# A ninth seven-product pair in the second row group of a two-group layer-1 product

## The chip, the cores and the metric

The kernel runs on one core of one Trainium2 chip. The metric is the device time of one execution in microseconds (us). A core has five engines that run on their own and wait for each other through semaphores: PE (TensorE, the matrix engine), DVE (VectorE), ACT (ScalarE), POOL (GpSimd) and SP (SyncE, which only issues transfers here). PEld is PE's loading of weights, which overlaps its multiplying. Transfers (DMAs) are issued from SP, and from POOL where they add to what lies at their target.

## The reference, cut to what matters

```python
def layer_norm(x):
    mu = jnp.mean(x, axis=-1, keepdims=True)
    sigma = jnp.sqrt(jnp.mean((x - mu) ** 2, axis=-1, keepdims=True))
    return (x - mu) / sigma
x1, x2 = x[:, :5120], x[:, 5120:]          # x: (1024, 10240)
h1 = leaky_relu(layer_norm(x1 @ W1.T))     # W1: (256, 5120)
h2 = leaky_relu(layer_norm(x2 @ W1.T))
h1 = leaky_relu(layer_norm(h1 @ W2.T))     # W2: (64, 256)
h2 = leaky_relu(layer_norm(h2 @ W2.T))
h = leaky_relu(layer_norm(jnp.concatenate([h1, h2], -1) @ W3.T))   # W3: (8, 128)
y = h @ W4.T                               # W4: (1, 8)
```

Nearly all of the work is the first product, with F = 5120 as the contracted dimension. The rest is called layers 2 to 4 below.

## The kernel before, in words

The rows are cut into two groups of 512. A group has B = 2 blocks of 512 columns b (256 rows times the two halves x1 and x2), W1 has M = 2 blocks of 128 outputs m. The contraction runs over PAIRS = 20 pairs of 128-element slices, so a pair is a 2 by 2 by 2 block product. It is done in one of two ways:

- A unit of kind E does the pair as eight block products. It has two parts (E0, E1), one for each slice, and each needs 4 products.
- A unit of kind S does it as seven (Strassen's way in Winograd's form). It has a part R (three products on blocks as they are loaded: A11, A12, S4 into banks P1, P2, P3) and a part T (four products on sums of blocks: S1, S3, S2, A22 into P5, P7, P6, P4). The sums of x are made on DVE (`two_sums` L758, `third_sum` L767, `fourth_sum` L777) in `x_sum`. For units with `added_by_dma` (L319, the third to the sixth S unit of the whole kernel) the first two of them are made by a DMA from POOL's queue that adds the block b12 to two loaded blocks (`add_b12`, L496).

Each product is made with three matmuls of 128 by 512, since float32 is split in a high and a low part: ACT casts to `_hi` (`hi`, L577), DVE subtracts to `_lo` (`lo`, L707), and PE multiplies hi by hi, lo by hi and hi by lo. An E unit is therefore 24 matmuls, an S unit 21 (R 9, T 12). The split buffers R, T, E0 and E1 are single: ACT casts into one only when PE has used it (`used`).

W1 is centred, summed and split once, in the first group, by ACT and DVE. A pair that is E in the first group and S in the second needs its weights a second time in the summed form. Those units are in `W_WORK` (L125): w is loaded again by SP (L471), centred by ACT (L566), summed by three DVE instructions (L743, L748, L753), cast by ACT (L575) and subtracted by DVE (L717). Before, two units of the second group need it.

The order of the units is written in ORDER (L46). F is the first unit of the second group, L the last of the first group, whose four (b, m) blocks are finished one after another, and D is the last of all, two E pairs in four parts, first for b = 0 and then for b = 1. All engines go through the same order in loops over `RUNS` (L130: a run is the E-like units between two S units, then an S unit). The run that crosses from group to group is written out by hand for ACT (L644) and DVE (L948): DVE adds up the seven products (`seven_into`, L797) and the eight (`eight_into`, L816) into h1, ACT makes the leaky ReLU and the squares (`leak1`, `square1`), PE makes layer 2 (L1152) right after F and layer 3 (L1183) after the unit behind F, ACT squares and casts layer 2's result (`layer2_end`), DVE copies layer 3's and the variances' bank out (`small`, L992), and PE may only start the bank P7 (before) when that copy is made (`free`, L1051). POOL folds the squares with a row of adding DMAs (L509 to L530) and raises to the power -1/2 (`root12`, `root3`); DVE ends the first group beside the unit named by `first_end` (L993).

In the names of units below, S7 is the first S unit of the second group (the seventh of all), S8 the next, and so on. Before, these are S7 to S14; E' is the E unit behind F, and the last units are S14, E, D.

Of the kernel before, what the change touches and what calls it, by code (L numbers as in the profile page):

```python
# [17 lines left out]
B = 2  # L18
# [8 lines left out]
MIXED = 2  # L27
# [7 lines left out]
EARLY = 2  # L35
E_RING = 4
W23_UNIT = 7
# [8 lines left out]
ORDER = ("EHE" + "SEE" * 3 + "SE" * 2 + "SEEL", "FE" + "SE" * 8 + "D")  # L46
# [39 lines left out]
def plan():  # L86
    units, made, halves, sevens = [], {}, 0, 0
    for g, order in enumerate(ORDER):
        seen = {"S": 0, "E": 0}
        for kind in order:  # L90
# [4 lines left out]
            else:  # L95
# [4 lines left out]
                elif kind in "HL":  # L100
                    wanted = [("T", pair, 0, (0, 1)), ("T", pair, 1, (0, 1))]
                elif kind == "D":
                    wanted = [("E0", pair, 0, (0, 1)), ("T", pair + 1, 0, (0, 1)), ("T", pair + 1, 1, (0, 1)),
                              ("E1", pair, 1, (0, 1))]
                else:
                    wanted = [("E0", pair, 0, (0, 1)), ("E1", pair, 1, (0, 1))]
# [15 lines left out]
SEVENS = [u for u in UNITS if u.kind == "S"]  # L122
HALVES = {part.half: part for u in UNITS if u.kind != "S" for part in u.parts}
# [32 lines left out]
def rec_kernel(nc, x, w1, w2, w3, w4, out):  # L156
    with ExitStack() as ctx:  # L157
# [36 lines left out]
        unused = sb("unused", [P, 2, N1], BF16)  # L194
        w2_raw = sb("w2_raw", [P, M, N2])
# [19 lines left out]
        sq3 = sb("sq3", [P, B * T, N3])  # L215
        a3 = sb("a3", [P, B * T, N3])
        weighted = sb("weighted", [P, B * T, N3])
        var3 = sb("var3", [P, B * T])
# [89 lines left out]

        def two_slot(u):


            return u.nth % S_RING, 16 * ((u.nth - EARLY) // S_RING + 1)

        def b12_slot(u):

            n = u.nth if u.nth < EARLY else u.nth - SEVEN + EARLY
            return u.nth % S_RING, 16 * (n // S_RING + 1)

        def added_by_dma(u):  # L319
            return EARLY <= u.nth < SEVEN  # L320
# [41 lines left out]
        def _(sp):  # L362
# [79 lines left out]
            for es, n, after in RUNS:  # L442
# [20 lines left out]
                if es[0].n == W23_UNIT:  # L463
                    sp.dma_start(w2_raw[:], w2).then_inc(small_landed, 16)
# [13 lines left out]
        def _(pool):  # L478
# [25 lines left out]
            for u in SEVENS[EARLY:SEVEN]:  # L504
                add_b12(u)
# [36 lines left out]
        def _(act):  # L542
            def mean(u, c):
                s, landed = w_slot(u)
                act.activation(unused[:, c, :], w_raw[:, s, c * N1:(c + 1) * N1], ACT.Copy, scale=-1.0 / N1,  # L545
# [57 lines left out]
            def layer1_end(g):  # L603
                for b in range(B):
                    for m in range(M):
                        leak1(g, b, m)
                for b in range(B):
                    for m in range(M):
                        square1(g, b, m)

# [27 lines left out]
            for i, (es, n, after) in enumerate(RUNS):  # L638
                if not n:
                    copy_p1(GROUPS - 1)  # L640
                    for part in es[1].parts:
                        hi(es[1], part)
                    break
                if crosses(es):  # L644
# [54 lines left out]
        def _(dve):  # L699
# [67 lines left out]
            def third_sum(u):  # L767
# [4 lines left out]
                else:  # L772
                    dve.wait_ge(two_sums_made, u.nth + 1 if u.nth < EARLY else u.nth + 1 - SEVEN + EARLY)
# [23 lines left out]
            def seven_into(g, k):  # L797
# [7 lines left out]
                if k == 1:  # L805
                    dve.wait_ge(h1_step, 2 * g + 1)
                    dve.tensor_tensor(h1[1][0], h1[1][1], acc[:, P5, :], ALU.add)
# [4 lines left out]
                if k == 3:  # L812
                    dve.wait_ge(h1_step, 2 * g + 2)
# [448 lines left out]
```

## Time and profile before

| | us |
|---|---|
| median of 3 runs | 230.14 |
| lowest and highest | 229.82 and 230.61 |
| the profiled execution | 229.74 |
| its span, from the first to the last instruction | 228.0 |
| PE busy | 222.1 (97%) |
| DVE busy | 193.9 (85%) |
| ACT busy | 152.1 (67%) |
| POOL busy | 27.9 (12%) |

The profiled execution is 229.74 us long, of which 228.0 us are the span and 1.7 us lie around it. Busy time says how long an engine had an instruction in work. For DVE and ACT two neighbouring instructions overlap in the listing by about 0.09 us, so the distance from start to start is what one costs in a row. A matmul is listed with some 0.39 us, but PE starts one every 0.23 us. The profile also has the granted clock of TensorE, which is 0.99 of full speed over the span.

### The profile page before, as it was taken

Reading aid. Unit: us, or ns where it says so; the run is one execution under the profiler, and the core shown is the slowest. Engines: PE = TensorE matmul, PEld = TensorE weight load, DVE = VectorE, ACT = ScalarE, POOL = GpSimd, SP = SyncE. Lnnn points to the kernel's source line nnn. Section 1 sums busy time; section 2 is a strip of 40 time slices with the busy share of each in tenths; the row PEclk is TensorE's granted clock in tenths of the full one; section 3 lists DMA queues with packets and bytes.
Section 4 is the critical chain, followed back from the end, with each engine's and each line's share of the span. In section 5 each row is a group of like instructions: output and inputs, shape, how many; then the busy total and the mean of one; then the engine's idle time right before and its main releaser. Section 6 shows DMA issues by size and latency. Waiting matters only on the chain.

```text
span 228.0 us, 2897 instructions
## 1 busy us (share of the span) xinstructions
PE 222.1 (97%) x991; PEld 178.6 (78%) x991; DVE 193.9 (85%) x264; ACT 152.1 (67%) x240; POOL 27.9 (12%) x41
## 2 busy tenths in 40 slices
PE   8999999999999999999999999999999999999992
PEld 2888877888888888888868888888888888888771
DVE  3789999959779999996669799998989999968564
ACT  4997989689498598963678363665545585616540
POOL 0000020200200200000012243227040000000014
PEclk9999999999999999999999999999999999999996
DMA  6999999999999998546738958567666815050000
GB/s 214 405 407 407 401 358 324 316 242 348 309 216 379 302 312 283 175 157 224 281 66 235 282 196 281 207 213 220 215 212 206 272 75 184 3 184 1 3 0 1
DMA packets 17950, 51.93 MB, mean 228 GB/s; under 512 B 2772, under 2 KB 3156, under 8 KB 17936
## 3 DMA queue, kind: packets, MB, share of 16 engines
q1 hardware_dynamic: 15920, 48.60, 60.7%
q0 software_dynamic: 1872, 2.89, 7.8%
q10 hardware_dynamic: 144, 0.26, 0.4%
q8 instruction: 8, 0.13, 0.2%
q14 instruction: 6, 0.05, 0.1%
HBM read 50.95 MB, written 0.01 MB: 224 GB/s over the span
## 4 chain that ended last, share of the span: by engine, by line
PE 83%; DVE 5%; ACT 4%; DMA 4%; issue 1%; POOL 1%; SPq 1%; POOLq 0%; DVEq 0%
PE acc L1037 80%; DMA xe_raw<-x 4%; PE acc L1158 2%; DVE xe_lo L709 2%; ACT xe_hi L591 2%; ACT unused L545 1%; DVE x_sum L764 1%; ACT xt_hi L591 1%; DVE x_sum L774 1%; ACT we_hi L551 0%; POOL inv L488 0%; PE acc L1171 0%; ACT stage L551 0%; PE acc L1187 0%; POOLq L157 0%
## 5 line engine op out<-in xcount | busy, mean ns | idle before, releaser
L1037 PE MATMUL acc<-xe_lo,we_hi 128*128 128x512 f32 x176 | 68.8, 391 | 0.3 <-DVE xe_lo L709 0.2
L1037 PE MATMUL acc<-xe_hi,we_lo 128*128 128x512 f32 x176 | 68.5, 389 | 0.0
L591 ACT CAST xe_hi<-xe_raw 128x1024 fp32r<-128x1024 f32 (+1 forms) x48 | 48.2, 1011 | 28.2 <-PE acc L1037 22.4
L709 DVE TENSOR_TENSOR xe_lo<-xe_raw,xe_hi 128x1024 fp32r<-128x1024 f32 (+1 forms) x48 | 55.5, 1178 | 12.3 <-ACT xe_hi L591 11.9
L1037 PE MATMUL acc<-xe_hi,we_hi 128*128 128x512 f32 x176 | 48.4, 391 | 0.0
L1037 PEld LDWEIGHTS acc<-xe_lo,we_hi 128*128 128x128 f32 x176 | 33.0, 188 | 8.4 <-issue 1.7
L1037 PEld LDWEIGHTS acc<-xe_hi,we_hi 128*128 128x128 f32 x176 | 32.9, 188 | 7.8 <-issue 1.1
L1037 PEld LDWEIGHTS acc<-xe_hi,we_lo 128*128 128x128 f32 x176 | 33.0, 188 | 6.7
L591 ACT CAST xt_hi<-x_sum 128x2048 fp32r<-128x2048 f32 x14 | 26.8, 1912 | 14.0 <-DVE x_sum L780 14.0
L709 DVE TENSOR_TENSOR xt_lo<-x_sum,xt_hi 128x2048 fp32r<-128x2048 f32 x14 | 32.1, 2290 | 1.9 <-ACT xt_hi L591 1.9
L1037 PE MATMUL acc<-xt_lo,ws_hi 128*128 128x512 f32 x64 | 25.0, 390 | 0.0
L1037 PE MATMUL acc<-xt_hi,ws_lo 128*128 128x512 f32 x64 | 24.9, 389 | 0.0
L591 ACT CAST xr_hi<-xs_raw 128x1536 fp32r<-128x1536 f32 x14 | 20.7, 1477 | 6.1 <-PE acc L1037 6.1
L709 DVE TENSOR_TENSOR xr_lo<-xs_raw,xr_hi 128x1536 fp32r<-128x1536 f32 x14 | 24.5, 1753 | 0.0
L1037 PE MATMUL acc<-xt_hi,ws_hi 128*128 128x512 f32 x64 | 17.1, 390 | 0.0
L1037 PE MATMUL acc<-xr_lo,ws_hi 128*128 128x512 f32 x42 | 16.5, 392 | 0.0
L1037 PE MATMUL acc<-xr_hi,ws_lo 128*128 128x512 f32 x42 | 16.4, 390 | 0.0
L545 ACT ACTIVATE unused<-stage 128x256 bf16<-128x256 f32 x39 | 15.8, 406 | 0.0
L1037 PEld LDWEIGHTS acc<-xt_lo,ws_hi 128*128 128x128 f32 x64 | 12.0, 188 | 2.7 <-issue 0.2
L1037 PEld LDWEIGHTS acc<-xt_hi,ws_hi 128*128 128x128 f32 x64 | 12.0, 188 | 2.5
L575 ACT CAST ws_hi<-stage 128x896 fp32r<-128x896 f32 x8 | 7.6, 944 | 9.6 <-DVE stage L753 9.6
L1037 PEld LDWEIGHTS acc<-xt_hi,ws_lo 128*128 128x128 f32 x64 | 12.0, 188 | 2.4
(112 smaller groups left out, 267.0 us busy)
## 6 DMA issues: line engine op xcount, KB each, us to landing
xe_raw<-x SPq DMA_DIRECT2D x51, 512.0 KB, 4.8
xs_raw<-x SPq DMA_DIRECT2D x14, 768.0 KB, 5.5
stage<-w SPq DMA_DIRECT2D x21, 256.0 KB, 5.6
x_sum<-x SPq DMA_DIRECT2D x10, 256.0 KB, 3.3
x_sum<-x SPq DMA_DIRECT2D x4, 512.0 KB, 4.3
x_sum<-x POOLq DMA_DIRECT2D x4, 512.0 KB, 8.5
stage<-w SPq DMA_DIRECT2D x2, 128.0 KB, 3.2
xe_raw<-x ACTq DMA_DIRECT2D x1, 256.0 KB, 3.3
```

Of the source, the lines that this page charges most:

```text
L545: act.activation(unused[:, c, :], w_raw[:, s, c * N1:(c + 1) * N1], ACT.Copy, scale=-1.0 / N1, accum_out=w_mean[:, u.pair, c:c + 1]).then_ ...
L575: act.copy(ws_hi[:, u.pair, :], w_mid[:, P:]).then_inc(w_hi_ready, 1)
L591: act.copy(hi_of(u, part), raw_of(u, part)).then_inc(hi_ready[part.buffer], 1)
L709: dve.tensor_tensor(lo_of(u, part), raw_of(u, part), hi_of(u, part).bitcast(F32), ALU.subtract)\
L764: dve.tensor_tensor(x_sum[:, s, 0:2 * NC].rearrange("p (a n) -> p a n", a=2), raw[:, 0:3:2, :], b12, ALU.add).then_inc(two_sums_made, 1)
L774: dve.tensor_tensor(x_sum[:, s, 2 * NC:3 * NC], x_sum[:, s, 0:NC], x_block(u, 2), ALU.add)\
L1037: return pe.matmul(acc[:, bank, :], w, x, start=first, stop=True, skip_group_check=True)
L1158: ins = pe.matmul(h2_ps[b][h * N2:(h + 1) * N2, :], w2_sb[:, m, :], a1[:, b, m, h * T * P:(h + 1) * T * P], start=(m == 0), stop=(m == M - ...
```

## The change

The second group gets nine S units instead of eight, and eleven pairs as E instead of twelve. Its order is now F, eight times S E, then S and D, where it was F, E, eight times S E, D. So an S unit follows F directly, and an S unit stands directly ahead of D. One more unit (now three) has its weights made a second time.

Along with that:

- The bank that holds layer 2's results for b = 0 and 1 moves from P1 and P5 to P5 and P7, the small results of the first group from P7 to P6, and `free` waits accordingly: P5 and P7 for ACT's reading of layer 2, P6 for DVE's copy to `small`.
- In the crossing run ACT and DVE take the end of the first group, F's parts and the next S unit's parts in another order. Layer 3 of the first group comes between the parts R and T of S7.
- The S units whose first two sums are added by DMA are now also the last three of the second group, S13, S14 and S15. DVE makes them for S7 to S12.
- DVE ends the first group beside S12 (before beside S11). POOL issues the adds for S13 ahead of its `root12` and `root3` for the first group, and those for S14 and S15 behind them.
- D's parts are taken as E0, E1, T, T instead of E0, T, T, E1, and the additions at the end are ordered anew. `seven_into_bank` adds the seven-product sums into the banks of b = 1.
- Three buffers are dropped: the unused output of ACT's `mean` now goes to the place that the cast fills later, `w2` is centred in place, and `sq3` shares with `weighted`.

```diff
-MIXED = 2
+MIXED = 3
...
-ORDER = ("EHE" + "SEE" * 3 + "SE" * 2 + "SEEL", "FE" + "SE" * 8 + "D")
+ORDER = ("EHE" + "SEE" * 3 + "SE" * 2 + "SEEL", "F" + "SE" * 8 + "SD")
...
+ADDED = (*range(2, SEVEN), *range(len(SEVENS) - MIXED, len(SEVENS)))
...
-        h2_ps = [acc[:, bank, 0:T * P] for bank in (P1, P5)]
+        h2_ps = [acc[:, bank, 0:T * P] for bank in (P5, P7)]
-        var2_bank = ((P7, P7), (P2, P7))
-        h3_bank = ((P7, P7), (P4, Q))
+        var2_bank = ((P6, P6), (P2, P1))
+        h3_bank = ((P6, P6), (P4, Q))
...
+            add_b12(SEVENS[-3])
             pool.wait_ge(consts_ready, 5)
             root12(1, 0, B)
             root3(1, 0, B)
+            add_b12(SEVENS[-2])
+            add_b12(SEVENS[-1])
...
@@ ACT, crossing run
-                    for part in es[3].parts:
-                        hi(es[3], part)
-                    layer1_end(es[0].g)
-                    for part in es[4].parts:
-                        hi(es[4], part)
-                    for b in range(B):
-                        layer2_end(es[0].g, b)
+                    g = es[0].g
+                    hi(es[3], es[3].parts[0])
+                    leak1(g, 0, 0)
+                    hi(es[3], es[3].parts[1])
+                    leak1(g, 0, 1)
+                    square1(g, 0, 0)
+                    square1(g, 0, 1)
+                    for m in range(M):
+                        leak1(g, 1, m)
+                        square1(g, 1, m)
                     hi(n, n.parts[0])
                     hi(n, n.parts[1])
+                    for b in range(B):
+                        layer2_end(g, b)
...
@@ DVE, last run
-                    for k in range(4):
-                        seven_into(g, k)
-                    for part in es[1].parts:
-                        lo(es[1], part)
-                    for m in range(M):
-                        seven_into_bank(m)
+                    seven_into(g, 0)
+                    seven_into(g, 1)
+                    for part in es[0].parts[2:]:
+                        lo(es[0], part)
+                    seven_into_bank(0)
+                    seven_into(g, 2)
+                    seven_into(g, 3)
+                    eight_into(g, 0, 0)
+                    eight_into(g, 0, 1)
+                    seven_into_bank(1)
                     break
@@ DVE, crossing run
-                    for part in es[3].parts:
-                        lo(es[3], part)
-                    for b in range(B):
-                        for m in range(M):
-                            eight_into(g, b, m)
-                    for b in range(B):
-                        sum_squares(g, b)
-                    for part in es[4].parts:
-                        lo(es[4], part)
-                    sums(n)
+                    lo(es[3], es[3].parts[0])
+                    for m in range(M):
+                        eight_into(g, 0, m)
+                    lo(es[3], es[3].parts[1])
+                    for m in range(M):
+                        eight_into(g, 1, m)
+                    sum_squares(g, 0)
+                    two_sums(n)
+                    sum_squares(g, 1)
+                    third_sum(n)
+                    fourth_sum(n)
                     lo(n, n.parts[0])
...
-                if crosses(es):
-                    dve.wait_ge(h3_summed, B)
-                    dve.tensor_copy(small[:, B * J:B * J + B * J * N3], h3_ps(0, 0, B)).then_inc(small_copied, 1)
-                first_end = n.nth == SEVEN + 4
+                first_end = n.nth == SEVEN + 5
...
                 lo(after[0], after[0].parts[0])
+                if crosses(es):
+                    dve.wait_ge(h3_summed, B)
+                    dve.tensor_copy(small[:, B * J:B * J + B * J * N3], h3_ps(0, 0, B)).then_inc(small_copied, 1)
...
@@ PE
+                    if bank in (P5, P7):
+                        pe.wait_ge(a2_ready, B * (g - 1) + {P5: 1, P7: 2}[bank])
                     if bank == P6:
-                        pe.wait_ge(drained, 5 * (g - 1) + 1)
-                    if bank == P7:
                         pe.wait_ge(small_copied, g)
...
+                    if u.n == len(FIRST) + 1 and part.buffer == "R":
+                        for b in range(B):
+                            layer3(0, b)
```

## Rows read from the trace of the kernel before

**Rows 1.** The page: busy time of each engine, and the last chain's shares by engine.
```profile
PE 222.1 (97%) x991; PEld 178.6 (78%) x991; DVE 193.9 (85%) x264; ACT 152.1 (67%) x240; POOL 27.9 (12%) x41
...
PE 83%; DVE 5%; ACT 4%; DMA 4%; issue 1%; POOL 1%; SPq 1%; POOLq 0%; DVEq 0%
```

**Rows 2.** The last chain in order of time: start, length, what (xcount instructions).
```profile
36.73 80.49 PE acc L1037 x353
...
125.55 89.91 PE acc L1037 x396
```

**Rows 3.** Groups by line and shape: out<-in xcount | busy us, mean ns | idle before.
```profile
L709 DVE TENSOR_TENSOR xe_lo<-xe_raw,xe_hi 128x1024 fp32r<-128x1024 f32 x44 | 52.9, 1223 | 12.1 <-ACT xe_hi L591 11.8 <-issue 0.2
...
L591 ACT CAST xe_hi<-xe_raw 128x1024 fp32r<-128x1024 f32 x44 | 45.8, 1046 | 26.4 <-PE acc L1037 22.4 <-DMA xe_raw<-x 3.8
...
L709 DVE TENSOR_TENSOR xt_lo<-x_sum,xt_hi 128x2048 fp32r<-128x2048 f32 x14 | 32.1, 2290 | 1.9 <-ACT xt_hi L591 1.9
```

**Rows 4.** Timeline of PE at the crossing: start, us, instruction, [idle before].
```profile
106.17 0.39 PE L1037 MATMUL acc<-xt_hi,we_hi 128*128 128x512 f32 x1
...
117.14 1.95 PE L1158 MATMUL acc<-x_sum,w_sb 128*64 128x256 f32 x16
119.02 1.20 PE L1037 MATMUL acc<-xe_hi,we_hi 128*128 128x512 f32 x4
...
124.59 0.96 PE L1187 MATMUL acc<-w_sb,stage 128*128 128x16 f32 x8
125.40 0.96 PE L1037 MATMUL acc<-xr_hi,ws_hi 128*128 128x512 f32 x3
```

**Rows 5.** Timeline of DVE at the crossing.
```profile
105.17 1.22 DVE L709 TENSOR_TENSOR xe_lo<-xe_raw,xe_hi 128x1024 fp32r<-128x1024 f32 x1
...
110.03 2.54 DVE L820 TENSOR_TENSOR stage<-acc,stage 128x512 f32<-128x512 f32 x4
...
126.39 0.22 DVE L992 COPY small<-acc 128x64 f32<-128x64 f32 x1
...
130.41 1.23 DVE L764 TENSOR_TENSOR x_sum<-xs_raw,x_sum 128x1024 f32<-128x1024 f32 x1 [1.53 <-DMA x_sum<-x]
```

**Rows 6.** Timeline of ACT at the crossing.
```profile
107.81 1.05 ACT L591 CAST xe_hi<-xe_raw 128x1024 fp32r<-128x1024 f32 x1 [2.95 <-DMA xe_raw<-x]
110.75 2.49 ACT L601 ACTIVATE x_sum<-stage 128x512 f32<-128x512 f32 x4 [1.89 <-DVE stage L820]
113.15 2.18 ACT L613 ACTIVATE stage<-stage 128x512 f32<-128x512 f32 x4
...
119.14 0.38 ACT L619 ACTIVATE stage<-acc 128x256 f32<-128x256 f32 x1 [0.20 <-PE acc L1158]
```

**Rows 7.** Timeline of DVE, a steady cycle: `two_sums` of S11.
```profile
158.63 1.22 DVE L764 TENSOR_TENSOR x_sum<-xs_raw,x_sum 128x1024 f32<-128x1024 f32 x1
```

**Rows 8.** DMA issues: all of a kind, then one from 60:62 us alone; KB, us to landing.
```profile
x_sum<-x SPq DMA_DIRECT2D x4, 512.0 KB, 4.3
x_sum<-x POOLq DMA_DIRECT2D x4, 512.0 KB, 8.5
...
x_sum<-x POOLq DMA_DIRECT2D x1, 512.0 KB, 9.6
```

**Rows 9.** Timelines of PE, DVE and ACT at the end.
```profile
201.71 1.07 PE L1037 MATMUL acc<-xe_hi,we_hi 128*128 128x512 f32 x4
...
201.91 0.69 DVE L804 TENSOR_TENSOR stage<-stage,acc 128x512 f32<-128x512 f32 x1 [1.49 <-PE acc L1037]
...
212.40 1.29 DVE L820 TENSOR_TENSOR stage<-acc,stage 128x512 f32<-128x512 f32 x2 [0.80 <-PE acc L1037]
...
215.43 0.69 DVE L838 TENSOR_TENSOR stage<-stage 128x512 f32<-128x512 f32 x1 [1.74 <-ACT stage L613]
...
219.31 0.16 DVE L849 TENSOR_TENSOR cancelled<-var_inverse,var 128x4 f32<-128x4 f32 x1
220.20 0.98 DVE L833 TENSOR_TENSOR stage<-stage,xs_raw 128x256 f32<-128x256 f32 x2 [0.72 <-ACT xs_raw L694]
```

More of the change, by code:

```diff
@@ L102, in plan @@
                 elif kind == "D":
-                    wanted = [("E0", pair, 0, (0, 1)), ("T", pair + 1, 0, (0, 1)), ("T", pair + 1, 1, (0, 1)),
-                              ("E1", pair, 1, (0, 1))]
+                    wanted = [("E0", pair, 0, (0, 1)), ("E1", pair, 1, (0, 1)), ("T", pair + 1, 0, (0, 1)),
+                              ("T", pair + 1, 1, (0, 1))]
                 else:
@@ L307, in w_slot, with added_by_dma, sevens_until, nth_of_slot @@
             return W_AT[u.n] % W_RING, 16 * (W_AT[u.n] // W_RING + 1)
+        def added_by_dma(u):
+            return u.nth in ADDED
+        def sevens_until(u, by_dma):
+            return [v for v in SEVENS[:u.nth + 1] if added_by_dma(v) == by_dma]
+        def nth_of_slot(u, by_dma):
+            return len([v for v in sevens_until(u, by_dma) if v.nth % S_RING == u.nth % S_RING])
         def two_slot(u):
-            return u.nth % S_RING, 16 * ((u.nth - EARLY) // S_RING + 1)
+            return u.nth % S_RING, 16 * nth_of_slot(u, True)
         def b12_slot(u):
[L316 to L320, printed above, removed]
+            return u.nth % S_RING, 16 * nth_of_slot(u, False)
         def raw_of_seven(u):
@@ L502, in add_b12 @@
                                accum_op=ALU.add).then_inc(two_sums_ready[s], 16)
-            for u in SEVENS[EARLY:SEVEN]:
+            for u in [v for v in SEVENS[:SEVEN] if added_by_dma(v)]:
                 add_b12(u)
@@ L544, in mean @@
                 s, landed = w_slot(u)
-                act.activation(unused[:, c, :], w_raw[:, s, c * N1:(c + 1) * N1], ACT.Copy, scale=-1.0 / N1,
+                act.activation(w_half_of_eight(w_his, u.pair, c), w_raw[:, s, c * N1:(c + 1) * N1], ACT.Copy, scale=-1.0 / N1,
                                accum_out=w_mean[:, u.pair, c:c + 1]).then_inc(w_mean_ready, 1)
@@ L640, in _ @@
                     copy_p1(GROUPS - 1)
-                    for part in es[1].parts:
-                        hi(es[1], part)
+                    for part in es[0].parts[2:]:
+                        hi(es[0], part)
                     break
@@ L805, in seven_into @@
                 if k == 1:
[L806 to L807 removed]
+                    dve.wait_ge(h1_step, 3 * g + 1)
+                    dve.tensor_tensor(h1[1][0], h1[1][1], acc[:, P5, :], ALU.add).then_inc(h1_step, 1)
                 if k == 2:
@@ L825, in seven_into_bank @@
                 bank = E_BANK[1][m]
-                dve.wait_ge(drained, 5 * (GROUPS - 1) + 1)
-                dve.wait_ge(used["E1"], UNITS[-2].parts[1].nth)
+                g = GROUPS - 1
+                if m == 0:
+                    dve.wait_ge(h1_step, 3 * g + 2)
+                else:
+                    dve.wait_ge(drained, 5 * g + 1)
+                dve.wait_ge(used["T"], UNITS[-2].parts[1].nth)
                 dve.tensor_tensor(acc[:, bank, :], acc[:, bank, :], h1[1][m], ALU.subtract).then_inc(added, 1)
@@ L1118, in first_eight @@
                     ins.then_inc(used[part.buffer], 1)
+                    if part.c == 0:
+                        pe.wait_ge(block_done, 4 * u.g)
+                        pe.sem_inc(used["T"], 2)
             def last_eight(u):
@@ L1199, in _ @@
                     first_eight(u)
-                    pe.wait_ge(block_done, 4 * u.g)
-                    pe.sem_inc(used["T"], 2)
                     pe.wait_ge(consts_ready, 5)
@@ L1212, in _ @@
                     eight(u)
-                if u.n == len(FIRST) + 1:
-                    for b in range(B):
-                        layer3(0, b)
             g = GROUPS - 1
```

26 lines of the change are left out of this document (7 added, 19 removed).

## The prediction, made before the changed kernel ran

> **What bounds the kernel now.** I read the busy times first: PE has work for 97% of the span, and the last chain is PE for 83% [rows 1]. The chain in order of time then says where [rows 2]: from 36.73 us on it never leaves PE until the end of layer 1, and behind the first group's layers it does 396 matmuls in 89.91 us, 0.2270 us each. No wait ends on PE in there. DVE (85%) and ACT (67%) only have to be in time. So in the second group a matmul less is worth 0.227 us, as long as what feeds PE stays ahead of it. Then I laid out the two places where the order changes, the crossing and the end, engine by engine [rows 4 to 6, 9], and a steady cycle [rows 7].
>
> **The gain.** A pair as seven products has 21 matmuls and as eight 24: 3 x 0.227 = 0.68 us less on PE. That is all that the change takes from the path.
>
> The Trainium skill (TensorE: Matmul & The Clock Gate, Back-to-back issue gap) gives about 131 ns for each matmul of 512 columns in a sustained stream. By it the gain would be 0.39 us; the trace says 227 ns for this stream [rows 2], so the row decides.
>
> **The crossing, PE.** Before, PE does F, layer 2 (from 117.14), E' (from 119.02), layer 3 (from 124.59) and S7 (from 125.40) [rows 4]. E' was 5.6 us of cover for the sums and splits of S7. After the change S7's part R starts at 119.02, its 9 matmuls end at 121.06, layer 3 takes the same 0.81 to 121.87, and part T starts its products into P5, P7 and P6 at 121.87, 122.10 and 122.32.
>
> **The crossing, DVE and ACT.** From start to start a 1024 subtraction is 1.13, a 2048 one 2.21, and a cast of 1024 0.95, by their means less 0.09 [rows 3]; a 512 addition out of a bank 0.62 [rows 5], a leak 0.61 and a square 0.54 [rows 6]. L, whose first matmul is at 106.17 [rows 4], ends a block each 1.36 us.
> - DVE splits F's first part at 105.17 as before [rows 5] and now adds block (0,0) at 107.65 and (0,1) at 109.0. ACT, which cast F's second part at 107.81 when its load had come [rows 6], does the first leak at 108.4 and that cast at 109.0; DVE splits it at 110.1, and PE wants it at 111.6 + 2.7 = 114.3.
> - DVE adds (1,0) and (1,1) at 111.2 and 111.8. ACT's leaks and squares of b = 1 then end at 114.4 (before 115.3), its cast of R at 115.8.
> - DVE: squares of b = 0 at 112.4, `two_sums` at 113.0, squares of b = 1 at 114.45, third and fourth sum to 116.45, split of R to 118.1. PE wants the split at 119.02 + 0.68 = 119.7: 1.6 us in hand.
> - ACT casts T at 116.5 to 118.4, DVE splits it to 120.7. PE wants it at 122.8: 2.1 us in hand.
> - P5 and P7 want ACT's readings of layer 2, the last of which waits for PE until 119.14 as before [rows 6] and ends at 119.8: free.
> - P6 wants the copy to `small`. It now stands on DVE behind the split of S7's follower E, whose cast ACT starts at 119.7, so that split runs from 120.8 to 121.95, and the copy also needs the last layer-3 matmul, about 122.0. It takes 0.22 [rows 5] and ends at 122.3, when PE's weight load for P6 is already due (a matmul time ahead of 122.32). I price this at 0.2 us. Its ends are 0 (PE loads and multiplies without a gap) and 1.13, one whole 1024 subtraction more in front of the copy. I take 0.2 because both conditions of the copy end within 0.1 us of each other.
> - S8: its b12 block waits behind a 768 KB load. Before, that pair let DVE start `two_sums` at 130.41 after a wait of 1.53, 5.2 us ahead of PE's S8 (135.6) [rows 5]. After, the two loads start some 5.6 us earlier, with R's split and layer 2's end, `two_sums` starts near 124.6, and PE's S8 is at 130.3: 5.7 us ahead. Cost nothing; with 1.5 us less it would begin to cost.
>
> **The steady cycles.** `two_sums` of S11 starts at 158.63 [rows 7], and PE's S11 at 125.40 + 4 x 45 x 0.227 = 166.26: 7.6 us ahead, as far as the single buffers let it. A cycle S E costs DVE 9.1 us of PE's 10.2, so after the crossing the distance grows from 5.7 to 7.6 in two cycles. With weights to make, the cycle costs DVE some 11.2 us in the trace of before; there are now three such cycles, but the DMA takes `two_sums` (1.22 [rows 7]) out of them, so they cost about 10.0 and no longer eat distance. The end of the first group beside S12 costs DVE 3 us once, as it did beside S11. Cost nothing, with 1.6 us in hand at the tightest (T of S13).
>
> **The adds by DMA.** Their loads are 512 KB and land after 4.3 us, the add itself after 8.5 in the median and 9.6 at most [rows 8], in a stretch where the load of the DMA engines is higher. The load for a unit may start when DVE has split T of the unit two before. For S15 that is at 182.6; loaded 186.9, added 193.8 to 196.5; `third_sum` is due at 194.75, and PE is not hurt before another 3.3 us. S14 has more in hand. POOL's queue: the add for S13 is issued near 164.4, and `root12` wants its turn near 171; the adds for S14 and S15 stand behind `root3` (about 175.0) and hold up nobody, since the next of POOL's instructions is at the very end. SP's queue: each of these loads is 256 KB longer, ahead of E halves that have a cycle in hand. The repeated weights of a third unit are 256 KB more, asked for near 164 and wanted at 195. Cost nothing.
>
> The Trainium skill (DMA: Bandwidth & Descriptors, Anatomy of one DMA — SWDGE path) prices a transfer from POOL's queue at about 2.0 us plus its bytes at 436 GB/s, 3.2 us for 512 KB. By it the adds could never be late and the third rival below would have no chance; the row of 9.6 us contradicts it, so the rival stays.
>
> **The end.** D's first matmul, D0, was at 201.71 + 24 x 0.227 = 207.15 [rows 9] and comes 0.68 less the loss at P6 earlier. Now S15 stands right ahead of it, so what DVE did beside the last E falls into D: D0 + 0.20 the first addition (the lag of 201.91 behind 201.71), D0 + 1.52 the split of the first T part (PE wants its end, D0 + 2.74, at D0 + 3.17), the second to D0 + 3.88 (wanted at + 4.53), the bank of (1,0) at D0 + 4.49 (wanted at + 5.44), then two more additions, and (0,0) at D0 + 5.86. Before, that one was at 212.40, D0 + 5.25. So the b = 0 results come 0.61 us later with respect to PE. Layer 2 for b = 0 wants them at D0 + 8.16, when they are 0.4 us old. DVE's variance chain, 215.43 to 219.47 before, shifts by the same 0.61, to D0 + 12.93, and what follows it on DVE waited for ACT until 220.20, D0 + 13.05 [rows 9]. So 0.61 of a cover of 0.73 us is used, and the path is still PE's. Cost nothing; with the cover gone, up to 0.6.
>
> The new place for ACT's unused output costs nothing: an instruction of the same shape and engine.
>
> **Sum.** -0.68 + 0.20 = -0.48 us. From the profiled execution's own 229.74 that is 229.26. The median of the runs stands 0.40 above that execution, so the same step from 230.14 gives 229.66; the likeliest is 229.6 us. A measurement of this kernel can tell about 0.3% (0.69 us) from no change, and the runs shown are spread over 0.79 us. So even the whole gain lies at the edge of what can be told.
>
> **Rivals.**
> - Whole gain: the copy is in time, P6 costs nothing. For it: both ends of that wait are estimates to 0.2 us. Time 230.14 - 0.68 = 229.46. Chance 0.27.
> - DVE ends last at the finish: the variance chain outlasts its cover. For it: only 0.12 us are left, against it that DVE's order there is fixed and has no load to wait for. It returns 0.3 to 0.6, 230.1. Chance 0.08.
> - An add by DMA is late: it decides from 11 us on for S15 (186.9 to 194.75 + 3.3), where the longest of the trace is 9.6, or from a late turn on POOL. A lateness of 1 us gives 230.6. Chance 0.04.
> - Slower: PE stands at the crossing for want of DVE and ACT. They now do in 111.6 to 122.3 what they had 5.6 us longer for, in turns: ACT waited 1.89 us for DVE and 2.95 for a load there [rows 6]. Each engine's queue is in order, so one late cast pushes T's split, the follower's split and the copy alike. If it is one E part on both engines, 1.13 + 0.95 = 2.1 us late against the schedule, PE loses about 1.9 at P6 and the time is 230.14 - 0.68 + 1.9 = 231.4. It decides from 0.5 us more than my 0.2 (then nothing is gained) and is slower by 0.3% from 1.4. Chance 0.14.
> - The change doesn't shorten PE's work at all: excluded by the plan, since S has 21 matmuls at the same pace as E.
> - My forecast has 0.44, and 0.03 is for what I don't see.
>
> **How the numbers follow.** Range 229.1 to 230.9: its low end is the whole gain less half the spread of the runs, its high end the forecast with P6 at its upper end of 1.13 and the runs' spread (230.6, and 0.3); the far half of the slower rival is left out. Faster by over 0.3% (below 229.45): half of the whole-gain case and a quarter of the forecast's, 0.25. Slower by over 0.3% (above 230.83): the crossing rival and little more, 0.15. Within: 0.60.
>
> **What would show it.** PE should have 915 matmuls of layer 1 and its second group no wait but one, of 0 to 0.4 us, ahead of the first product into P6. The copy to `small` should start within 0.2 us of layer 3's last matmul. `two_sums` of S8 should be 5 us or more ahead of PE, `third_sum` of S14 and S15 wait for a DMA by at most 1.8. At the end the wait ahead of the last additions of squares (L833 before) should shrink from 0.72 to about 0.1. It is wrong if PE's waits in the second group sum to over 0.7, if the matmuls' pace changes, or if the first 117 us, which should stay as they are, move.

## The result, and the profile after

| | before, us | after, us |
|---|---|---|
| median of 7 runs | 230.14 | 229.45 |
| lowest and highest | 229.77 and 230.61 | 229.26 and 229.68 |
| the profiled execution | 229.74 | 229.57 |
| its span | 228.0 | 227.8 |

The ratio is 0.9965, with a 95% interval of 0.9949 to 0.9981: 0.69 us less, inside the range of 229.1 to 230.9 and just at the bound of 0.3% that I had set for a difference. The number is that of the rival "whole gain" (229.46) and not of my forecast (229.6). The range holds the time of before as well, so the time alone shows little, and the medians fix the gain only between 0.44 and 1.17 us.

The page of after, its busy times and the shares of the last chain, which answers to [rows 1]:

```profile
PE 221.7 (97%) x988; PEld 178.6 (78%) x988; DVE 196.3 (86%) x268; ACT 155.1 (68%) x243; POOL 32.4 (14%) x44
...
PE 82%; DVE 5%; DMA 4%; ACT 4%; issue 1%; POOL 1%; SPq 1%; POOLq 0%; DVEq 0%
```

PE has three matmuls less. DVE and ACT have 2.4 and 3.0 us more to do, for the ninth S unit and its weights, and POOL 4.5, most of it for issuing three more adds (1.2 us each). The last chain of after in order of time (start, length, what, xcount), which answers to [rows 2]:

```profile
36.99 80.48 PE acc L1051 x353
117.47 1.88 PE acc L1179 x16
...
122.41 92.64 PE acc L1051 x408
...
225.20 0.16 DVE y L910
```

The steady stretch of the first group is as long as before (80.48 and 80.49 us). It starts at 36.99 and not at 36.73. That start moves from run to run of one and the same kernel, and so does the whole execution with it: a second profile of the unchanged kernel after had 36.65, another kernel with the same code up to there had 38.11. In that stretch the path is only PE, so a better measure than the time of one execution is the distance from this start to the last `y`. Before it was 188.89 us (36.73 to 225.62), after it is 225.20 - 36.99 = 188.21: 0.68 us less, which is three matmuls of 0.227 us to the last digit. I call this distance the stretch from here on. It is free of what the first loads do; it comes from a single execution each, but five such profiles, of after (twice) and of three variants of it (below; in two of them this path was expected to stay as it is, in the third it turned out to), lie between 188.19 and 188.29.

### The profile page after: what moved, and what is told of

Its sections match the earlier page's. It is cut to its first block, busy times and chain, and to the rows that moved or that the text cites. A ratio compares the mean times of both kernels' runs of the same rounds, so it can differ in the third digit from the quotient of the medians.

```text
span 227.8 us, 2907 instructions
## 1 busy us (share of the span) xinstructions
PE 221.7 (97%) x988; PEld 178.6 (78%) x988; DVE 196.3 (86%) x268; ACT 155.1 (68%) x243; POOL 32.4 (14%) x44
## 4 chain that ended last, share of the span: by engine, by line
PE 82%; DVE 5%; DMA 4%; ACT 4%; issue 1%; POOL 1%; SPq 1%; POOLq 0%; DVEq 0%
PE acc L1051 80%; DMA xe_raw<-x 4%; PE acc L1179 2%; DVE xe_lo L716 2%; ACT xe_hi L601 2%; DVE x_sum L771 1%; ACT xt_hi L601 1%; ACT we_hi L555 1%; DVE x_sum L781 1%; ACT we_hi L561 0%; POOL inv L494 0%; PE acc L1192 0%; ACT stage L561 0%; ACT ws_hi L555 0%; PE acc L1208 0%
## 5 line engine op out<-in xcount | busy, mean ns | idle before, releaser
L1051 PE MATMUL acc<-xe_lo,we_hi 128*128 128x512 f32 x160 | 62.6, 391 | 0.3 <-DVE xe_lo L716 0.2
L1051 PE MATMUL acc<-xe_hi,we_lo 128*128 128x512 f32 x160 | 62.3, 389 | 0.0
L601 ACT CAST xe_hi<-xe_raw 128x1024 fp32r<-128x1024 f32 (+1 forms) x46 | 46.1, 1010 | 23.0 <-PE acc L1051 19.9
L716 DVE TENSOR_TENSOR xe_lo<-xe_raw,xe_hi 128x1024 fp32r<-128x1024 f32 (+1 forms) x46 | 53.2, 1175 | 9.1 <-ACT xe_hi L601 8.9
L1051 PE MATMUL acc<-xe_hi,we_hi 128*128 128x512 f32 x160 | 43.9, 390 | 0.0
L1051 PEld LDWEIGHTS acc<-xe_lo,we_hi 128*128 128x128 f32 x160 | 30.0, 188 | 7.8 <-issue 1.7
L716 DVE TENSOR_TENSOR xt_lo<-x_sum,xt_hi 128x2048 fp32r<-128x2048 f32 x15 | 34.3, 2288 | 1.9 <-ACT xt_hi L601 1.9
L1051 PEld LDWEIGHTS acc<-xe_hi,we_hi 128*128 128x128 f32 x160 | 30.0, 188 | 6.8 <-issue 0.7
L1051 PEld LDWEIGHTS acc<-xe_hi,we_lo 128*128 128x128 f32 x160 | 30.0, 188 | 6.1
L506 POOL DMA_DIRECT2D x_sum<-x x7 | 8.6, 1236 | 86.6 <-DMA x_sum<-x 86.6
```

Of the source, the lines that this page charges most:

```text
L506: pool.dma_start(x_sum[:, s, 0:2 * NC].rearrange("p (a n) -> p a n", a=2), b12_of(u).rearrange("p (o n) -> p o n", o=1).broadcast_to([P, 2 ...
L601: act.copy(hi_of(u, part), raw_of(u, part)).then_inc(hi_ready[part.buffer], 1)
L716: dve.tensor_tensor(lo_of(u, part), raw_of(u, part), hi_of(u, part).bitcast(F32), ALU.subtract)\
L1051: return pe.matmul(acc[:, bank, :], w, x, start=first, stop=True, skip_group_check=True)
```

## Where the wait went: the crossing of after

Timeline of PE at the crossing, which answers to [rows 4]:

```profile
119.28 0.96 PE L1051 MATMUL acc<-xr_hi,ws_hi 128*128 128x512 f32 x3
...
121.45 0.96 PE L1208 MATMUL acc<-w_sb,stage 128*128 128x16 f32 x8
122.26 1.20 PE L1051 MATMUL acc<-xt_hi,ws_hi 128*128 128x512 f32 x4
...
125.13 1.07 PE L1051 MATMUL acc<-xe_hi,we_hi 128*128 128x512 f32 x4
```

and of PE's weight load and DVE there, which answers to [rows 5]:

```profile
122.72 0.30 PEld L1051 LDWEIGHTS acc<-xt_hi,ws_hi 128*128 128x128 f32 x2 [0.19 <-DVE small L1017]
...
118.76 2.29 DVE L716 TENSOR_TENSOR xt_lo<-x_sum,xt_hi 128x2048 fp32r<-128x2048 f32 x1 [0.30 <-ACT xt_hi L601]
...
122.45 0.22 DVE L1017 COPY small<-acc 128x64 f32<-128x64 f32 x1 [0.20 <-PE acc L1208]
...
125.01 1.23 DVE L771 TENSOR_TENSOR x_sum<-xs_raw,x_sum 128x1024 f32<-128x1024 f32 x1 [1.21 <-DMA x_sum<-x]
```

The schedule that I had laid out by hand held. S7's T runs four matmuls without a gap from 122.26. The copy to `small` ends 1.22 us behind the start of layer 3 (122.67 - 121.45; predicted 122.3 - 121.06 = 1.24). The weight load for P6 does wait, 0.19 us. The matmul into P6 does not: T's twelve matmuls take 125.13 - 122.26 = 2.87 us, 0.15 more than 12 x 0.227, but R behind layer 3 lost nearly as much before, where nothing waited (from 125.40 to its fourth matmul 0.79 us, and 3 x 0.227 is 0.68). Two kernels below put this reading to the test.

## The experiments

**An unchanged kernel.** The kernel after once more, beside the first experiments.

> The changed kernel itself, to stand beside the others on one chip. Only the count of matmuls (my theory): 0.68 us less than the kernel before, and the trace again has the copy to small as the last thing that the product into P6 waits for, with no loss on PE. Rival (part of the gain is lost at P6): 0.5 us less.

Measured: 229.71 us against 230.16 of before, ratio 0.9969 [0.9947, 0.9991]. Its stretch is 188.29. So the gain is there again, 0.3% and no more, and this is the kernel to set the next ones against.

**Is it the count of matmuls, or the new order?** The order of after at the crossing and the end, but with eight S units in the second group, so that a pair has its 24 matmuls back.

```diff
-MIXED = 3
+MIXED = 2
-ORDER = (..., "F" + "SE" * 8 + "SD")
+ORDER = (..., "F" + "SEE" * 2 + "SE" * 5 + "SD")
-ADDED = (*range(2, SEVEN), *range(len(SEVENS) - MIXED, len(SEVENS)))
+ADDED = (*range(2, SEVEN), *range(len(SEVENS) - 3, len(SEVENS)))
```

> Undoes the count alone: eight units of seven in the second group, in the changed kernel's order (one right behind F, one right ahead of D), with its banks and its queues; the twelfth E pair goes into the middle (F, twice S E E, five times S E, S D). Theory that only the count matters: PE does the same matmuls as the kernel before, so 230.1 us, ratio 1.000 to the kernel before, 0.68 above the changed kernel. Rival that the new order at the crossing and at the end gives a part of the gain: 229.5 to 229.9.

Measured: 238.6 us, ratio 1.0343 [1.0299, 1.0386]. It was not the clean experiment that I had meant. The unit beside which DVE ends the first group is counted from the front (S12 here as in after). The unit whose add stands ahead of `root12` on POOL is counted from the back: with one S unit less it is S12 and no longer S13, so the add for S13 now stands behind `root12`. Timeline of POOL in that kernel:

```profile
167.76 1.22 POOL L506 DMA_DIRECT2D x_sum<-x  x1 [4.54 <-DMA x_sum<-x]
183.08 2.52 POOL L494 TENSOR_TENSOR inv<-var,minus_half 128x8 f32<-128x8 f32 x1 [14.10 <-DVE var L884]
...
187.60 2.49 POOL L506 DMA_DIRECT2D x_sum<-x  x2
```

POOL stood 14.10 us at `root12` with two adds behind it. The same kernel with that taken away (no third add, and the first group ended one unit earlier):

```diff
-ADDED = (*range(2, SEVEN), *range(len(SEVENS) - 3, len(SEVENS)))
+ADDED = (*range(2, SEVEN), *range(len(SEVENS) - MIXED, len(SEVENS)))
...
-            add_b12(SEVENS[-3])
...
-                first_end = n.nth == SEVEN + 5
+                first_end = n.nth == SEVEN + 4
```

> Eight units of seven in the changed kernel's order once more, with the fault of the first try taken out: there the add for S13 stood on POOL's queue behind the powers of the first group's end beside S12, was issued at 187.6 though its load had landed near 177, and DVE waited 6.4 us for it. Now S13 and S14 alone are added by DMA and the first group ends beside S11, a unit earlier, so that each add stands behind the powers as in the changed kernel. Theory (only the count of matmuls matters): PE does what it did in the kernel before, ratio 1.000 to it, 230.1, and 188.9 us from PE's first steady matmul at 37 us to the last y. Rival (the new order itself gives a part of the gain): 229.5 to 229.9, 188.2 to 188.6 us.

Measured: 230.23 us against 230.13, ratio 1.0005 [0.9992, 1.0019]. The row of its chain that answers to the 408 matmuls of after:

```profile
122.47 93.32 PE acc L1050 x411
```

411 matmuls in 93.32 us, where after has 408 in 92.64: 0.68 us for three. The stretch, from 37.01 to 225.95, is 188.94, that of before 188.89. So the new order at both ends neither gives nor costs anything within the 0.1 us that the stretches can tell, and the whole gain is three matmuls.

**Is the wait at P6 one that can cost?** The copy to `small` stands one 1024 subtraction later on DVE, the upper end that I had given for this wait.

```diff
-                if crosses(es):
-                    dve.wait_ge(h3_summed, B)
-                    dve.tensor_copy(small[...], h3_ps(0, 0, B)).then_inc(small_copied, 1)
...
                 lo(after[0], after[0].parts[1])
+                if crosses(es):
+                    dve.wait_ge(h3_summed, B)
+                    dve.tensor_copy(small[...], h3_ps(0, 0, B)).then_inc(small_copied, 1)
```

> The changed kernel with DVE's copy to small moved behind the second subtraction of the E unit that follows the first unit of seven, one 1024 subtraction further. It measures the wait at P6 and its price. Theory (the copy is the only thing that P6 waits for, and in the changed kernel PE has next to no reserve there): the copy starts at about 123.3 instead of 122.45, the product into P6 about 1.0 us later, all of it lost: 1.0 us above the changed kernel. Rival (there is cover that I did not see, or PE catches up later): less than 0.4.

Measured: 230.42 us, ratio 1.0007 [0.9983, 1.0032], and a stretch of 189.08, 0.87 above after. Timelines of DVE and PE:

```profile
124.33 0.22 DVE L1021 COPY small<-acc 128x64 f32<-128x64 f32 x1
...
123.28 0.72 PE L1051 MATMUL acc<-xt_hi,ws_hi 128*128 128x512 f32 x2
124.60 0.72 PE L1051 MATMUL acc<-xt_hi,ws_hi 128*128 128x512 f32 x2 [0.60 <-DVE small L1021]
```

The copy comes 0.86 us later with respect to layer 3 (1.86 us behind its start at 122.47, in after 1.00), and all of it is lost within the 0.1 us that the stretches can tell: with this one subtraction more, the gain of the whole change is gone. The wait is real, and in after it had hardly anything in hand.

**Does it cost anything in after?** P6 taken as the last of T's four products instead of the third, which gives the copy a matmul more time.

```diff
-                    for k, (n, bank) in enumerate(products):
+                    in_order = list(enumerate(products))
+                    if u.n == len(FIRST) + 1 and part.buffer == "T":
+                        in_order = [in_order[k] for k in (0, 1, 3, 2)]
+                    for k, (n, bank) in in_order:
```

> The changed kernel, but in T of the first unit of seven the product into P4 is taken ahead of the one into P6. It takes the wait for the copy off PE. Theory (the wait costs nothing, since the first matmuls behind the small ones of layer 3 lose 0.12 us anyway): T still takes 2.87 us from its first matmul to the next unit's. Rival (the wait costs 0.1 to 0.2): 2.72 to 2.77.

Measured in one run: 230.38 us, with the steady stretch starting at 37.81, and a stretch of 188.19, that of after to 0.02. Timeline of PE:

```profile
123.06 1.19 PE L1051 MATMUL acc<-xt_hi,ws_hi 128*128 128x512 f32 x4
...
125.92 1.07 PE L1051 MATMUL acc<-xe_hi,we_hi 128*128 128x512 f32 x4
```

T takes 2.86 us, against 2.87. So P6 costs 0.0 in after (0.01 by these two numbers), and the 0.15 belongs to the first matmuls behind a small product, before and after alike.

**Are the adds by DMA needed?** The last three sums on DVE and no add in the second group.

```diff
-ADDED = (*range(2, SEVEN), *range(len(SEVENS) - MIXED, len(SEVENS)))
+ADDED = tuple(range(2, SEVEN))
...
-            add_b12(SEVENS[-3])
...
-            add_b12(SEVENS[-2])
-            add_b12(SEVENS[-1])
```

> The changed kernel without the three adds by DMA in the second group: DVE makes the first two sums of S13 to S15 itself (1.22 us each). In the changed kernel T of S13 is split at 183.6 and PE wants it at about 184.5, and the three cycles cost DVE 9.2 us. Theory (the adds are what lets the last three units pass unseen): a cycle then costs DVE 10.4 against PE's 10.2, T of S13 comes 0.4 late and the next two 0.2 more each: PE waits 0.6 to 1.0 us in all, 230.1 to 230.5. Rival (DVE has reserve enough without them): PE waits nothing, 229.45.

Measured: 229.88 us against 230.01, ratio 1.0000 [0.9985, 1.0015], and a stretch of 188.70, 0.49 above after: somewhat less than expected, and at another item. Its chain, and then the timelines of DVE and PE at S13:

```profile
172.41 2.53 POOL inv L494
...
183.57 33.09 PE acc L1048 x144
```
```profile
182.43 1.09 DVE L721 TENSOR_TENSOR ws_lo<-stage,ws_hi 128x896 fp32r<-128x896 f32 x1
...
182.65 0.84 PE L1048 MATMUL acc<-xr_hi,ws_hi 128*128 128x512 f32 x3
183.57 0.50 PE L1048 MATMUL acc<-xr_lo,ws_hi 128*128 128x512 f32 x1
```

PE waits for the low part of S13's weights, not for the split of T that I had called the tightest. The chain runs back from there through DVE to `root12`, which took 2.53 us. At S14 and S15 PE had no wait: with the sums on DVE a cycle costs it 10.2 us (the first weight sum of S13 and of S14 start at 177.68 and 187.90), as much as PE, and not the 10.4 that I had expected.

**Why does `root12` take 2.5 us?** In before it took 1.67 us, in after it takes 2.52, and DVE waits for it (rows below). One theory (A) was a conflict with the DVE subtraction that had started just ahead of it, the other that adding DMAs slow POOL down. The kernel with no add in this group (above) has 2.52 too. In this one DVE starts the subtraction only when `root12` is done:

```diff
+                if first_end:
+                    dve.wait_ge(inv12_ready, 1)
                 w_lo(after[0])
                 lo(after[0], after[0].parts[0])
```

> The changed kernel, but DVE waits for the power on POOL (root12) ahead of the subtraction that runs beside it. The power took 2.52 us there and 1.67 in the kernel before. Theory A (a GpSimd instruction that starts while DVE is in an instruction with two SBUF inputs waits for it): with DVE idle it takes 1.67. Theory B (the adding DMA issued ahead of it on POOL's queue, still landing, makes it long): 2.5 again. PE's time hardly changes in either, under 0.3 us.

Measured in one run: 229.67 us, a stretch of 188.21, that of after. Timelines of POOL and DVE, of this kernel, then of after, then of before:

```profile
171.42 1.67 POOL L494 TENSOR_TENSOR inv<-var,minus_half 128x8 f32<-128x8 f32 x1 [5.00 <-DVE var L884]
...
173.13 1.22 DVE L716 TENSOR_TENSOR xe_lo<-xe_raw,xe_hi 128x1024 fp32r<-128x1024 f32 x1 [1.85 <-POOL inv L494]
```
```profile
171.33 2.52 POOL L494 TENSOR_TENSOR inv<-var,minus_half 128x8 f32<-128x8 f32 x1 [3.77 <-DVE var L884]
...
171.09 1.22 DVE L716 TENSOR_TENSOR xe_lo<-xe_raw,xe_hi 128x1024 fp32r<-128x1024 f32 x1
173.88 0.23 DVE L892 TENSOR_TENSOR half<-small,inv 128x64 f32<-128x64 f32 x1 [1.57 <-POOL inv L494]
```
```profile
166.31 1.67 POOL L488 TENSOR_TENSOR inv<-var,minus_half 128x8 f32<-128x8 f32 x1 [7.66 <-DVE var L873]
...
166.41 1.23 DVE L709 TENSOR_TENSOR xe_lo<-xe_raw,xe_hi 128x1024 fp32r<-128x1024 f32 x1 [0.24 <-issue]
```

Where the subtraction starts 0.24 us ahead of `root12`, the power is 0.85 us longer, about what the subtraction still has to run (171.09 + 1.13 - 171.33 = 0.89). Where it starts behind it, by 0.10 us or by 1.71, the power takes 1.67. Theory A holds. In ten profiles, after among them, the subtraction starts just ahead of the power, and it takes 2.52 in all ten, with adds in this group or without. The Trainium skill (SBUF — State Buffer, SBUF: two separate sides) says that GpSimd and a VectorE instruction with two inputs in SBUF exclude each other for a whole instruction, whoever starts first; POOL's side of that is what these rows show. DVE's side they do not: the subtraction of before, started 0.10 us behind the power, is listed with its usual 1.23 us.

**What if S13's add stood behind `root3`?** This asks what the place of that add on POOL is worth.

```diff
-            add_b12(SEVENS[-3])
             pool.wait_ge(consts_ready, 5)
             root12(1, 0, B)
             root3(1, 0, B)
+            add_b12(SEVENS[-3])
             add_b12(SEVENS[-2])
```

> The changed kernel with one line moved: on POOL's queue the add for S13 stands behind the two powers of the first group's end, not ahead of them. Nothing else changes. Theory (POOL takes its queue in order, and the powers wait for DVE beside S12): the add is issued at about 176 instead of 166, lands 6 to 8 us later, third_sum of S13, due at 177.3, waits 5 to 7 us, and with 0.9 us in hand PE loses 4 to 6 us: 233.5 to 235.5. Rival (the add may come late, since DVE has 5 us of lead): under 1 us.

Measured in one run: 239.17 us, a stretch of 196.90, 8.7 above after and well beyond what I had expected. Timelines of POOL, DVE and PE, then a table by stretches (start:end, length, busy times with counts, granted clock, DMA share, GB/s):

```profile
176.79 2.52 POOL L506 DMA_DIRECT2D x_sum<-x  x2
...
184.81 0.69 DVE L781 TENSOR_TENSOR x_sum<-x_sum,xs_raw 128x512 f32<-128x512 f32 x1 [6.54 <-DMA x_sum<-x]
...
186.73 0.96 PE L1051 MATMUL acc<-xr_hi,ws_hi 128*128 128x512 f32 x3 [4.07 <-ACT ws_hi L585]
189.03 0.80 PE L1051 MATMUL acc<-xr_lo,ws_hi 128*128 128x512 f32 x1 [1.34 <-DVE ws_lo L724]
```
```profile
184.00:188.00 4.00, 0.96 (x3) 0.48 (x3) 3.19 (x5) 2.26 (x2) 0.00 (x0) 0.98 0.75 135
188.00:192.00 4.00, 2.97 (x7) 2.39 (x8) 4.00 (x3) 3.19 (x5) 0.00 (x0) 0.50 0.55 197
```

The add lands 8 us behind its issue and DVE waits 6.54 us for it. PE should have started S13's R at 182.51 and starts it at 186.73 (4.2 lost), then the three matmuls to 189.03 take 2.30 us instead of 0.68 (1.6 lost). The rest is the clock. Behind that pause the granted clock is 0.50, 1.2 instead of 2.4 GHz, and the 13 matmuls from 189.03 to 194.72 take 5.69 us instead of 2.95 (2.7 lost). The sum is 8.6 us of the 8.7. I had priced the waits only. The first kernel of eight S units lost 8.0 us in the same way and for the same reason: its stretch is 196.97, that of the same kernel with its adds free 188.94.

**How much cover is left at the end?** One more addition of 128x512 out of a bank, into a place that nobody reads, ahead of the last two seven-product additions (`seven_into(g, 2)` and the next) on DVE. It adds work and leaves nothing out.

```diff
                     seven_into_bank(0)
+                    dve.tensor_tensor(x_sum[:, ..., 0:NC], h1[1][1], acc[:, P7, :], ALU.add)
                     seven_into(g, 2)
```

> The changed kernel with one more addition of 128 by 512 out of a bank on DVE, 0.60 us, ahead of the last two seven-product additions of the end; its result goes to free memory. It measures what cover DVE has left at the end. Theory (0.15 us is left ahead of the last additions of squares, and layer 2 for b = 0 is not reached by the delay): the variance chain ends last and the time is 0.60 - 0.15 = 0.45 above the changed kernel. Rival (DVE's chain there is not the bound even then): under 0.15.

Measured: 229.46 us against 230.01, ratio 0.9976 [0.9960, 0.9992], and a stretch of 188.26, 0.05 above after. The expected 0.45 did not come. Timelines of after (DVE, ACT) and then of this kernel (DVE):

```profile
219.46 0.16 DVE L860 TENSOR_TENSOR cancelled<-var_inverse,var 128x4 f32<-128x4 f32 x1
219.78 0.98 DVE L844 TENSOR_TENSOR stage<-stage,xs_raw 128x256 f32<-128x256 f32 x2 [0.15 <-ACT xs_raw L701]
...
219.89 0.41 ACT L701 ACTIVATE xs_raw<-acc 128x256 f32<-128x256 f32 x1
```
```profile
220.03 0.16 DVE L860 TENSOR_TENSOR cancelled<-var_inverse,var 128x4 f32<-128x4 f32 x1
220.11 0.76 DVE L844 TENSOR_TENSOR stage<-stage,xs_raw 128x256 f32<-128x256 f32 x2
```

DVE's chain came 0.57 us later (220.03 against 219.46). In after, the pair of L844 has a wait inside it as well, which a listing by pairs hides: its second instruction needs the second L701, which ends at 220.30. That is why the pair takes 0.98 us there and 0.76 here. Most of the delay goes into the two waits, 0.11 us of it is left at the pair's end (220.87 against 220.76), and PE does not see that: its products behind it start at 220.62 here and at 220.65 in after. From D's first matmul (207.15 in before, 206.73 in after, 206.70 here) to the last `y` it is 18.47 us in all three, so the end costs nothing in any of them. How much more than this one addition the cover could take was not measured.

**One S unit more in the first group instead?** Seven S units in the first group, two with weights made a second time: nine in the second group as in after, and 21 matmuls for one more pair of the first. The last three units stay added by DMA, and the small weights are centred one unit later.

```diff
-SEVEN = 6
-MIXED = 3
+SEVEN = 7
+MIXED = 2
-ORDER = ("EHE" + "SEE" * 3 + "SE" * 2 + "SEEL", ...)
+ORDER = ("EHE" + "SEE" + "SE" * 5 + "SEEL", ...)
...
```

> A further pair of seven in the first group instead of the weights of a third pair made again: seven units of seven in the first group and nine in the second, sixteen in all where the changed kernel has fifteen (first group E H E, S E E, five times S E, S E E L; the centring of the small weights one unit later; two pairs have their weights made again in the second group). Theory (a matmul less is 0.227 us as long as DVE and ACT keep up; DVE costs about 10.1 us in a cycle S E of the first group, PE 10.2): another 0.68 less, 228.8. Rival (with four more S E cycles in a row DVE, ACT or the loads fall behind, since a cycle S E E gave them 5.4 us of PE's time to catch up): PE waits in the first group, and the time is 229.5 to 231.

> Sixteen units of seven (seven in the first group) again, for a trace: the profiled execution of the first try was disturbed on every engine. Theory (the first group can carry a seventh): 188.21 - 0.68 = 187.5 us from PE's first steady matmul at 37 us to the last y, and no wait of PE in the first group. Rival (DVE, ACT or the loads fall behind with four more S E cycles in a row): PE's waits in the first group sum to 0.7 us or more.

Measured: 231.49 us with one disturbed execution among the ten, 231.33 (229.61 to 232.78) without it, ratio 1.0029 [0.9996, 1.0061] to before, from which it can't be told apart. The second profile, of a single run, has 233.02. From its page, the shares of its chain; from its chain in order of time, an item of the first group; then timelines of PE and DVE there:

```profile
PE 55%; DVE 25%; DMA 12%; ACT 3%; issue 1%; POOL 1%; SPq 1%; POOLq 0%; DVEq 0%; ACTq 0%
```
```profile
57.48 10.94 DMA x_sum<-x
```
```profile
38.43 0.47 PE L1051 MATMUL acc<-xe_lo,we_hi 128*128 128x512 f32 x1
...
72.73 0.50 PE L1051 MATMUL acc<-xr_lo,ws_hi 128*128 128x512 f32 x1 [0.96 <-DVE ws_lo L724]
...
68.51 0.69 DVE L781 TENSOR_TENSOR x_sum<-x_sum,xs_raw 128x512 f32<-128x512 f32 x1 [3.30 <-DMA x_sum<-x]
```

PE's share of the chain falls from 82 to 55%, and DVE and the DMAs take its place. Layer 2 starts at 120.74 (in after 117.40) and `y` ends the chain as much later, so all of the loss lies ahead of the crossing. It is not the whole 3.3 us, though. The steady stretch starts at 38.43 here and at 36.99 in after, so the stretch is 190.10 us, 1.9 above after, where 0.7 less was expected. The medians give 1.6 (231.33 against 229.71 of after, measured beside it).

The loss begins with one add that took 10.94 us to land and for which DVE waited 3.30 us, until 68.51. Up to there PE does not wait in its steady stretch. Behind it PE waits for DVE at 72.73, and again at 84.00 (0.77 us). DVE could not make up for the late add: a cycle S E costs it 10.0 us there, where it also makes the weights of every pair (two such cycles start at 54.47 and 64.47), of PE's 10.2. So the same step that is worth 0.68 us in the second group costs 1.9 in the first, in that execution. Whether the first group could carry it with every add in time was not tried.

## Why the prediction was right or wrong

- **The gain, 0.68 us: right.** Three matmuls at the steady pace, measured twice: after against before (-0.68 in the stretch), and the new order with and without the ninth S unit (188.94 against 188.21). That the medians differ by 0.69 is luck in the last digit. The two profiled executions differ by 0.17 only, since what lies ahead of the steady stretch and behind the last `y` moves too (0.26 and about 0.2 us more in after). It is the stretch that shows the gain. By the 131 ns for a matmul that the Trainium skill gives (TensorE: Matmul & The Clock Gate, Back-to-back issue gap) the gain would have been 0.39, an estimate. The traces disagree with it: this stream ran at 227 ns again (408 in 92.64 us).
- **The loss at P6, 0.20 us: mis-sized, it is 0.0.** This is the step that failed. The times of the copy and of the load were right to 0.02 us; what I left out is that a weight load that waits 0.19 us need not make its matmul late, and that the matmuls behind layer 3 start slowly anyway. Where the load waited 1.04 us, in the kernel with the late copy, the matmul did wait (0.60). I gave the case without a loss 0.27 and my own 0.44. On estimates good to 0.2 us that was too fine a distinction, and the lower end should have had at least as much.
- **Upper end of that wait, 1.13: right in kind.** The late copy cost 0.87.
- **The hand schedule of the crossing: right.** Its start is 0.26 us later than I counted; with that taken off, R's split (116.71, counted 116.45), T's (118.76, 118.5) and `two_sums` of S8 (125.01, 124.6) are where I put them within 0.2 us. The slower rival, a late engine at the crossing, did not come up.
- **The steady cycles: no cost is right, the numbers under it are wrong.** I gave a cycle with weights some 11.2 us of DVE in before; that trace has 10.2 (the first weight sums of its two such units start at 179.88 and 190.10). So with an add by DMA it takes 9.2 (`stage` of S13 to S15: 176.61, 185.82, 195.03), not 10.0. But DVE waited 1.57 us for the longer `root12` (0.39 in before), which I had not in the sum. The split of T for S13 ended at 183.63 and PE wanted it at 184.51: 0.9 us in hand, not 1.6. The kernel with the sums on DVE lost 0.49 there.
- **The adds: cost right, the tight one was another.** I had looked at S15, landed at 188.68 + 5.5 = 194.2 (I had said 193.8 to 196.5) and used at 195.69. The tightest is S13's, issued at 166.34 (I had said 164.4) and landed 9.9 us later at 176.2, and used at 177.27. It is the longest of the adds, as the view of DMA issues of single stretches of after shows (KB, us to landing; the first is S13's, the second S15's):

```profile
x_sum<-x POOLq DMA_DIRECT2D x1, 512.0 KB, 9.9
...
x_sum<-x POOLq DMA_DIRECT2D x1, 512.0 KB, 5.5
```

- **A late turn on POOL** was in my third rival, at "1 us gives 230.6". The mechanism is right and its price was too low: one place later in the queue made DVE wait 6.5 us and cost 8.7, 2.7 of it by the clock, for which I had no term.
- **The end: schedule right, cover too small.** The addition that completes block (0,0) was at D0 + 5.83 (212.56 - 206.73, predicted 5.86), and the wait ahead of the squares' additions was 0.15 us (predicted about 0.1). What I called the rest of the cover was only its visible part: another 0.57 us cost nothing from D's first matmul to the last `y`. So the rival of the DVE chain ending last had less behind it than I said.
- **The chances.** 0.31 and 0.35% faster, with intervals that reach from 0.1 to 0.5%, lies on the bound between "faster" and "same". The split of 0.25 and 0.60 is neither confirmed nor refuted; with P6 at nothing, the two should have been near each other.

## What to carry to other kernels

Where one engine carries the path without a gap, a matmul saved is worth its pace and nothing else. What decides is whether each cover survives, and that is read off a schedule laid out by hand, instruction by instruction; at the crossing it held to 0.3 us. A difference of 0.3% is better read from a stretch inside the trace, between two instructions of the same path, than from the times of whole executions. On a queue that is served in order, a transfer belongs ahead of an instruction that waits for another engine, and an index counted from the back and one counted from the front should not be trusted to stay in that order when the count changes. A late weight load and a wait inside a pair that is listed as one row are both easily misread, the first as a loss and the second as no cover.

## What the runs showed of the hardware

- The same power on POOL (128x8) took 1.67 us, and 2.52 where a DVE subtraction of two SBUF tensors had started 0.24 us ahead of it.
- After 4.1 us without a matmul and three matmuls in the next 2.3, the granted clock was 0.50 for some 5 us, and matmuls came 0.43 instead of 0.227 us apart.
- An adding DMA of 512 KB took between 5.5 and 9.9 us to land in one execution, and 10.9 once in another kernel. Plain loads of that size from SP took 4.7 (`x_sum`) and 5.2 us (`xe_raw`) in the median.
- The first matmuls behind a small product lost 0.11 to 0.15 us, in every kernel of this case that was read there.
- The start of the steady stretch lay between 36.65 and 38.11 us for one and the same code ahead of it. That spread alone is twice the gain that was to be measured.
